# A ring of gathered rows with four hands in place of three, in a graph and attention layer

## The chip, the cores and the metric

The kernel runs on one core of a Trainium2 chip. The metric is the device time of one execution in microseconds (us). The kernel before has a median of 1078.74 us over three runs.

## The reference

The layer takes 3125 nodes with 256 features and 53,125 weighted edges, and it adds three things to `x`:

```
xn = layernorm(x)
x  = x + segment_sum(w * xn[dst], src) @ W.T + b    # edges: a gather, a sum by node, a product
       + mix(xn)                                    # linear attention over all nodes, norm, MLP, norm
x  = x + ffn(layernorm(x))                          # the two best of eight experts, then a norm
```

The attention needs a sum over all nodes (keys by values) before any node can be finished, so it has two passes over the nodes.

## The kernel before

**Tiles.** The nodes are 25 tiles of 128 rows. `x` stays in SBUF as `X`. The work has four stages. First the normalised rows times `W.T` are written to DRAM as `xg_dram`, while TensorE, VectorE, ScalarE and GpSimd sort the edges by target tile. The sort leaves a table of 444 columns (`COLS`). A column is a chunk: up to 128 edges whose targets lie in one tile. `SIX` holds the row of `xg_dram` for each edge, `SLO` the target's place in its tile and `SW` the weight. The first pass over the nodes (loop A, 13 steps of a pair of tiles, the last of one tile) and the second (loop B, the same) follow, and last comes the expert stage.

**The chunks ride along.** The 444 chunks are worked off beside loops A and B, with 18 chunks to a step (a round), which is three hands of six (`HAND`, `HANDS`, `RC`). Four engines take part:

- GpSimd issues one indirect DMA for each chunk (`gather`, line 572). It fills slot `c mod 18` of `RING`, 128 rows of 256 floats. Before it overwrites the first slot of a pair it waits for the pair of chunks that lay there 18 chunks earlier (`chunk_mm`, line 578). It does nothing else in loops A and B.
- VectorE makes a selection matrix `SEL` for each chunk (`select`), two hands ahead.
- TensorE multiplies `SEL` by the ring's slot (`hand`, line 1511, the product at line 1523). Two chunks share a PSUM bank, and the pairs alternate between banks 6 and 7. A hand waits until its six gathers have landed (`gathered[h]`) and until its `SEL` is there. A pair waits until VectorE has added the last pair but one to `X` (`x_added`).
- VectorE adds each product to its tile of `X` (`add`, line 1057), in the order of the chunks.

**Order of work.** Each engine has a fixed program order, and the hands stand between the parts of the loops. In loop B TensorE's step is: hand 0, the second projection of the step before (`b_project`), two pairs of hand 1, the attention of the next step (`b_attend`), the last pair of hand 1, a transpose, hand 2, and the hidden layer (`b_hidden`, line 1607). So whatever delays one of these delays all that stands behind it on TensorE, and ScalarE and VectorE wait for their inputs from it.

**Queues.** The gathers are issued by GpSimd on a queue of their own. SyncE loads the experts' first weights, one expert after each full round of chunks (`sp.wait_ge(chunk_mm[0], (e + 1) * (RC // 2))`, line 473).

Of the kernel before, what the change touches and what calls it, by code (L numbers as in the profile page):

```python
# [5 lines left out]
def gps_layer_program(nc, x, row, col, weight, gnn_wT, gnn_b, qkv_wT, ln1_g, ln1_b, mix_w1T, mix_b1,  # L6
# [12 lines left out]
    P = 128  # L19
    N, C = out.shape  # L20
# [21 lines left out]
    assert CQ <= P and CH <= P // 2 and QS4 * TILES <= 512 and 2 * SETS * TILES + TILES <= 512 and NG // 2 * TILES <= 512  # L42
    HAND = 6
    HANDS = 3
    RC = HANDS * HAND
    ROUNDS = 2 * PAIRS
    COLS = -(-(EK + TILES - 1) // HAND) * HAND
    TAIL = COLS // HAND - ROUNDS * HANDS
    assert TAIL == 2 and COLS <= 512
# [9 lines left out]
    with ctx:  # L59
        def sb(name, shape, dt=f32):  # L60
            return scope.enter_context(nc.sbuf_tensor(name, shape, dt))

        def sem(name):
            return ctx.enter_context(nc.semaphore(name))
# [51 lines left out]

        BID = sb("BID", [1, ROUNDS + 1, -(-RC // 4) * 4], i32)
        VX = sb("VX", [P, 2, CC, VE])
# [61 lines left out]
        scope.close()  # L180
        scope = until_ffn
        QT = sb("QT", [P, CC, TILES * P])
        RING = sb("RING", [P, RC, C])
        SEL = sb("SEL", [P, 2, HAND, P])


# [56 lines left out]
        bank = [ctx.enter_context(nc.psum_tensor(f"bank{n}", [P, 512], f32)) for n in range(8)]  # L243
# [50 lines left out]
        table_done = sem("table_done")  # L294
        slots_ready = sem("slots_ready")
        x_biased = sem("x_biased")
        gathered = [sem(f"gathered{h}") for h in range(HANDS)]
        sel_ready = sem("sel_ready")
        chunk_mm = [sem(f"chunk_mm{s}") for s in range(2)]
        x_added = sem("x_added")  # L300
# [137 lines left out]
        def _(sp):  # L438
# [33 lines left out]
            for e in range(NE):  # L472
                sp.wait_ge(chunk_mm[0], (e + 1) * (RC // 2))
                sp.dma_start(FW1A[:, e, :, :], exp_w1[e, :, :].rearrange("(c p) f -> p c f", p=P)).then_inc(up_in, 16)
# [21 lines left out]
        def _(pool):  # L496
# [74 lines left out]

            def gather(c):

                r, at = divmod(c, RC)
                k = at % HAND
                if r and k % 2 == 0:
                    pair = (c - RC) // 2
                    pool.wait_ge(chunk_mm[pair % 2], pair // 2 + 1)
                pool.indirect_dma_start(RING[:, at, :], None, xg_dram,  # L579
                                        bass.IndirectOffsetOnAxis(ap=SIX[:, c:c + 1], axis=0)  # L580
                                        ).then_inc(gathered[at // HAND], 16)
# [4 lines left out]
            for c in range(COLS):  # L586
                gather(c)
# [249 lines left out]
        def _(dve):  # L837
# [119 lines left out]
            def column_buckets():  # L957
                dve.wait_ge(bid_sum, 1)
                whole = ROUNDS * RC
                chain.link(V.tensor_scalar(BID[0:1, 0:ROUNDS, 0:RC], bank[6][0:1, 0:whole].rearrange("p (r c) -> p r c", c=RC),  # L960
# [98 lines left out]
            def hand(base, r, h, ks=range(HAND)):  # L1059

                t = r * HANDS + h
                for k in ks:
# [310 lines left out]
        def _(pe):  # L1373
            T = nc.tensor
# [11 lines left out]
            for b in range(TILES):  # L1386
                pe.wait_ge(oh_made, b + 1)
                for s in range(QS4):
                    ins = T.matmul(bank[6][0:CQ, s * TILES + b:s * TILES + b + 1], OH[:, b, s * CQ:(s + 1) * CQ], onesb[:, 0:1],
                                   start=True, stop=True)  # L1390
# [30 lines left out]
            for s in range(QS4 - 1):  # L1421
                lo, n = 2 * (s + 1), SETS - 2 * (s + 1)
                sets = CNT[0:CQ, s:s + 1, :].to_broadcast([CQ, n, TILES])
                for kind in range(2):
                    at = (kind * SETS + lo) * TILES
# [85 lines left out]
            def hand(r, h, js=range(HAND // 2)):  # L1511

                t = r * HANDS + h
                for j in js:
                    pair = t * (HAND // 2) + j
                    if j == 0:
                        pe.wait_ge(sel_ready, t + 1)
                        pe.wait_ge(gathered[h], r * (16 * HAND) + 16 * HAND)
                    if pair >= 2:
                        pe.wait_ge(x_added, 2 * (pair - 1))  # L1520
                    for u in range(2):
                        k = 2 * j + u
                        ins = T.matmul(bank[6 + pair % 2][:, u * C:(u + 1) * C], SEL[:, t % 2, k, :], RING[:, h * HAND + k, :],  # L1523
                                       start=True, stop=True)
                    ins.then_inc(chunk_mm[pair % 2], 1)

# [37 lines left out]
            for i in range(PAIRS):  # L1564
                a_transpose(i, (0, 1))
                hand(i, 0)
                a_project(i, (0, 1))
                hand(i, 1)
                hand(i, 2)
                a_outer(i, (0, 1))  # L1570
# [111 lines left out]
            for c in range(CC):  # L1682
                ins = T.matmul(bank[5][:, 2 * NE + c:2 * NE + c + 1], MEANR[0:1, c * P:(c + 1) * P], ones[0:1, 0:1], start=True, stop=True)
            ins.then_inc(mean_turned, 1)
            pe.wait_ge(mean_col, 1)
            for c in range(CC):
                ins = T.matmul(bank[5][0:1, 0:NE], MEAN[:, c:c + 1], RW[:, c, :], start=(c == 0), stop=(c == CC - 1))
# [104 lines left out]
```

## Time and profile before

| | us |
|---|---|
| runs of the kernel before | 1075.21, 1078.74, 4162.33 |
| median | 1078.74 |
| the profiled execution's own time | 1080.07 |
| its span, first to last instruction | 1078.2 |
| gathers, first to last issue | 211.7 to 871.6 |
| GpSimd busy, of the span | 571.1 (53%) |
| TensorE busy, of the span | 814.6 (76%) |
| VectorE busy, of the span | 674.9 (63%) |
| granted TensorE clock, mean | 0.882 |

Times of rows are counted from the start of the span. A row of the timeline gives start, length, engine and line, what is written and read, and in brackets how long the engine had been idle and what ended that. "remote" there means that the profile saw a semaphore's wait end and found no instruction that ended at that moment; on one core no other core can be meant. The ends of TensorE's matmuls are modelled in this profile, and their starts are recorded. PE is TensorE, PEld its weight loads, DVE is VectorE, ACT is ScalarE and POOL is GpSimd. One product of a chunk is two MATMUL records.

### The profile page before, as it was taken

The page shows a single profiled execution, that of the slowest core. Times are in us where ns is not written, and L with a number is a line of the kernel's source. Part 1 is how long each engine was busy: PE and PEld are TensorE (multiplying, and loading weights), DVE is VectorE, ACT ScalarE, POOL GpSimd, SP SyncE. Part 2 cuts the span into 40 slices and gives each one's busy share as a digit, 9 for nine tenths or more (in the row PEclk, how much of TensorE's full clock was granted, in tenths as well). Part 3 has the DMA queues.
Part 4 walks back from the last instruction along what each step waited for, and adds up shares of the span by engine and source line. Part 5 has one row for each costly group of instructions (what it writes and reads, how often), then busy time and mean ns, then how long its engine had stood idle before and what let it go on. Part 6 is the DMA issues. An engine that isn't in the chain of part 4 may idle for free.

```text
span 1078.2 us, 14388 instructions
## 1 busy us (share of the span) xinstructions
PE 814.6 (76%) x4349; PEld 648.0 (60%) x4349; DVE 674.9 (63%) x1932; ACT 375.3 (35%) x909; POOL 571.1 (53%) x624
## 2 busy tenths in 40 slices
PE   5887999845776686667666667666676778999997
PEld 4666899633554454445445555555555563899997
DVE  8888888514444454445445666666666677976685
ACT  1548999310211221111112222222222234756552
POOL 3824444276666666666665666666666620243342
PEclk9988999967979878887878888888888899999999
DMA  8110000032324332333332333333233440100000
GB/s 234 60 64 1 1 0 0 10 103 87 107 83 117 88 110 86 109 91 112 91 105 74 109 92 108 88 88 87 84 88 88 81 42 1 51 25 26 20 26 28
DMA packets 39177, 77.29 MB, mean 72 GB/s; under 512 B 9875, under 2 KB 22600, under 8 KB 39112
## 3 DMA queue, kind: packets, MB, share of 16 engines
q0 software_dynamic: 21312, 58.22, 19.8%
q1 hardware_dynamic: 17800, 18.29, 5.4%
q8 instruction: 30, 0.49, 0.2%
q14 instruction: 35, 0.29, 0.1%
HBM read 70.00 MB, written 6.48 MB: 71 GB/s over the span
## 4 chain that ended last, share of the span: by engine, by line
PE 44%; DVE 19%; another core or an unknown queue 19%; issue 11%; ACT 3%; DVEq 1%; POOL 1%; DMA 1%; SPq 0%; POOLq 0%; ACTq 0%
PE bank L1696 12%; PE bank L1486 9%; PE bank L1523 9%; DVE X L1057 8%; PE bank L1545 2%; PE bank L1618 2%; DVE SEL L1045 2%; PE bank L1404 1%; DVE ST L862 1%; PE bank L1377 1%; PE bank L1492 1%; PE bank L1493 1%; PE bank L1665 1%; PE bank L1621 1%
## 5 line engine op out<-in xcount | busy, mean ns | idle before, releaser
L579 POOL DMA_INDIRECT RING<-xg_rows,SIX x444 | 429.2, 967 | 246.5 <-issue 119.3
L1523 PE MATMUL bank<-RING,SEL 128*128 128x256 f32 x888 | 270.8, 447 | 191.9 <-DVE X L1057 153.6
L1057 DVE TENSOR_TENSOR X<-bank,X 128x256 f32 x444 | 187.2, 422 | 303.1 <-remote 205.7
L1523 PEld LDWEIGHTS bank<-RING,SEL 128*128 128x128 f32 x888 | 183.6, 220 | 257.7 <-DVE X L1057 187.3
L1045 DVE TENSOR_SCALAR SEL<-iota,SLO,SW 128x128 f32<-128x128 f32 x444 | 151.4, 343 | 0.0
L1486 PEld LDWEIGHTS bank<-OI,AS 128*128 128x128 f32 x832 | 97.4, 196 | 14.6 <-DVE AS L1014 9.5
L1486 PE MATMUL bank<-OI,AS 128*128 128x128 f32 x832 | 97.6, 279 | 8.8 <-DVE AS L1014 8.8
L566 POOL TENSOR_TENSOR AS<-LH,EPC 128x832 f32<-128x832 f32 x32 | 50.0, 1582 | 72.3 <-DVE LH L1006 72.3
L704 ACT ACTIVATE NK<-bank 128x256 f32<-128x256 f32 x25 | 9.7, 387 | 158.4 <-remote 127.8
L663 ACT ACTIVATE LD<-iota,LANE 128x128 f32<-128x128 f32 x208 | 62.5, 387 | 4.4 <-DVE LANE L994 4.0
L827 ACT ACTIVATE HF<-bank,FB 128x256 f32<-128x256 f32 (+1 forms) x104 | 49.5, 476 | 39.4 <-PE bank L1696 35.6
L1696 PE MATMUL bank<-QH,W1L 128*128 128x256 f32 (+1 forms) x208 | 59.5, 286 | 1.7 <-DVE W1L L1280 1.7
L597 POOL TENSOR_TENSOR RS<-VE,mhalf 128x1 f32<-128x1 f32 x25 | 15.5, 618 | 82.4 <-DVE VE L1330 82.4
L1696 PE MATMUL bank<-QH,W1H 128*128 128x256 f32 (+1 forms) x208 | 58.6, 282 | 0.0
L1696 PE MATMUL bank<-QL,W1H 128*128 128x256 f32 (+1 forms) x208 | 58.6, 282 | 0.0
L1696 PE MATMUL bank<-W2H,HFL 128*128 128x256 f32 x200 | 56.7, 283 | 0.0
L1696 PE MATMUL bank<-W2L,HFH 128*128 128x256 f32 x200 | 56.4, 282 | 0.0
L1696 PE MATMUL bank<-W2H,HFH 128*128 128x256 f32 x200 | 56.3, 282 | 0.0
L1545 PE MATMUL bank<-QKVW,XT 128*128 128x512 f32 x100 | 54.8, 698 | 0.0
L592 POOL TENSOR_TENSOR XN<-XN,B2C 128x256 f32<-128x256 f32 x25 | 20.0, 801 | 63.1 <-DVE B2C L1311 63.1
L1318 DVE TENSOR_TENSOR HFL<-HF,HFH 128x256 fp32r<-128x256 f32 (+1 forms) x104 | 47.6, 506 | 4.8 <-ACT HFH L827 4.2
L697 ACT COPY XT<-bank 128x512 f32<-128x512 f32 (+1 forms) x13 | 7.4, 569 | 121.7 <-remote 87.1
(273 smaller groups left out, 1491.0 us busy)
## 6 DMA issues: line engine op xcount, KB each, us to landing
RING<-xg_rows,SIX POOLq DMA_INDIRECT x444
FW1A<-in_exp_w SPq DMA_DIRECT2D x8, 512.0 KB
xg_rows<-XGS SPq DMA_DIRECT2D x12, 256.0 KB, 2.1
out<-YO SPq DMA_DIRECT2D x24, 128.0 KB, 1.7
X<-in_x SPq DMA_DIRECT2D x1, 1664.0 KB, 12.7
X<-in_x SPq DMA_DIRECT2D x1, 1536.0 KB, 8.3
FW<-in_exp_w SPq DMA_DIRECT2D x2, 512.0 KB, 4.5
QKVW<-in_qkv_wT SPq DMA_DIRECT2D x1, 768.0 KB
```

What stands on the lines that cost most here:

```text
L566: pool.tensor_tensor(AS[:, s, :, LC:2 * LC], LH[:, s, :, :], per_chunk(EPC, i, s, LC), ALU.mult).then_inc(ap_ready, 1)
L579: pool.indirect_dma_start(RING[:, at, :], None, xg_dram, bass.IndirectOffsetOnAxis(ap=SIX[:, c:c + 1], axis=0)).then_inc(gathered[at // HA ...
L663: ins = act.activation(LD[:, k, :], iota[:, :], ACT.Abs, scale=-1.0, bias=LANE[:, bass.ds((4 * i + s) * GC + k, 1)])
L827: ins = act.activation(into, bank[s][:, 0:width], ACT.Gelu, bias=FB1[:, n // FJ, n % FJ:n % FJ + 1])
L1045: ins = V.tensor_scalar(SEL[:, t % 2, k, :], iota[:, :], SLO[:, at], SW[:, at], ALU.is_equal, ALU.mult)
L1057: V.tensor_tensor(xt, bank[6 + pair % 2][:, half * C:(half + 1) * C], xt, ALU.add).then_inc(x_added, 1)
L1318: V.tensor_tensor(HFL[par][:, n, 0:width], HF[:, s, 0:width], HFH[par][:, n, 0:width].bitcast(f32), ALU.subtract).then_inc(hl_ready, 1)
L1486: ins = T.matmul(bank[s][:, 0:P], AS[:, s, k, :], OI[:, s, k, :], start=(k == 0), stop=(k == GC - 1))
L1523: ins = T.matmul(bank[6 + pair % 2][:, u * C:(u + 1) * C], SEL[:, t % 2, k, :], RING[:, h * HAND + k, :], start=True, stop=True)
L1545: ins = T.matmul(bank[2 + s][:, :], XT[:, c, s, :], QKVW[:, c, C:3 * C], start=(c == 0), stop=(c == CC - 1))
L1618: T.matmul(bank[3 + s][:, 0:C], HS[:, h, s, :], W2[:, h, :], start=(h == 0), stop=False)
L1696: ins = T.matmul(into, left, right, start=(m == 0), stop=(m == len(terms) - 1))
```

## The change

The ring gets a fourth hand: `RING` has 24 slots (24 KB in each partition) in place of 18. The hands of a round stay three, so hand `t` now lies in part `t mod 4` of the ring, and `gathered` becomes four semaphores. The gather of chunk `c` waits for the pair that held its slots 24 chunks earlier. SyncE's waits, `SEL`, the PSUM banks, the pairs and the order of work on every engine stay as they are.

```
     HAND = 6
     HANDS = 3
+    HELD = 4
     RC = HANDS * HAND
...
-        RING = sb("RING", [P, RC, C])
+        RING = sb("RING", [P, HELD * HAND, C])
...
-        gathered = [sem(f"gathered{h}") for h in range(HANDS)]
+        gathered = [sem(f"gathered{h}") for h in range(HELD)]
...
             def gather(c):
-                r, at = divmod(c, RC)
-                k = at % HAND
-                if r and k % 2 == 0:
-                    pair = (c - RC) // 2
+                lap, at = divmod(c, HELD * HAND)
+                if lap and at % 2 == 0:
+                    pair = (c - HELD * HAND) // 2
                     pool.wait_ge(chunk_mm[pair % 2], pair // 2 + 1)
                 pool.indirect_dma_start(RING[:, at, :], None, xg_dram,
...
             def hand(r, h, js=range(HAND // 2)):
                 t = r * HANDS + h
+                lap, held = divmod(t, HELD)
                 for j in js:
                     pair = t * (HAND // 2) + j
                     if j == 0:
                         pe.wait_ge(sel_ready, t + 1)
-                        pe.wait_ge(gathered[h], r * (16 * HAND) + 16 * HAND)
+                        pe.wait_ge(gathered[held], (lap + 1) * 16 * HAND)
...
-                        ins = T.matmul(bank[6 + pair % 2][:, u * C:(u + 1) * C], SEL[:, t % 2, k, :], RING[:, h * HAND + k, :],
+                        ins = T.matmul(bank[6 + pair % 2][:, u * C:(u + 1) * C], SEL[:, t % 2, k, :], RING[:, held * HAND + k, :],
                                        start=True, stop=True)
```

## Rows read from the trace of the kernel before

**Rows 1.** The page, part 1: busy us (share of the span) x instructions
```profile
PE 814.6 (76%) x4349; PEld 648.0 (60%) x4349; DVE 674.9 (63%) x1932; ACT 375.3 (35%) x909; POOL 571.1 (53%) x624
```

**Rows 2.** Waits, GpSimd's: us in total, times, longest us
```profile
POOL RING L579 <- issue: 119.3, 391, 0.5
...
POOL RING L579 <- remote: 67.5, 30, 4.1
...
POOL RING L579 <- PE bank L1523: 44.8, 22, 8.8
```

**Rows 3.** Line 579, the gathers: ns min/median/max, first and last start us
```profile
L579 POOL DMA_INDIRECT RING<-xg_rows,SIX x444: 940/946/1922, 211.7 to 871.6; - x148
```

**Rows 4.** Waits, TensorE's: the two on the ring's products
```profile
PE bank L1523 <- DVE X L1057: 153.6, 54, 13.2
...
PE bank L1523 <- DMA RING<-xg_rows,SIX: 8.5, 1, 8.5
```

**Rows 5.** Windows of line 579: stretch, its us, busy us (x gathers begun)
```profile
205.00:231.60 26.60, 15.32 (x16) 0.74 0.27 72
...
205.00:331.20 126.20, 81.28 (x83) 0.80 0.32 89
...
205.00:738.10 533.10, 344.50 (x356) 0.83 0.33 96
```

**Rows 6.** Windows of line 1523: the same stretches, PE busy (x matmuls)
```profile
205.00:231.60 26.60, 5.46 (x12) 3.96 (x13) 0.74 0.27 72
...
205.00:331.20 126.20, 45.52 (x144) 31.02 (x145) 0.80 0.32 89
...
205.00:738.10 533.10, 210.48 (x684) 143.74 (x685) 0.83 0.33 96
```

**Rows 7.** Timeline: the first product that reads the ring
```profile
221.20 5.46 PE L1523 MATMUL bank<-RING,SEL 128*128 128x256 f32 x12 [8.52 <-DMA RING<-xg_rows,SIX]
```

**Rows 8.** Timeline: the first long stall, in loop A
```profile
229.96 1.89 PE L1552 MATMUL bank<-XT,QKVW 128*128 128x256 f32 x8
...
231.68 1.89 PE L1523 MATMUL bank<-RING,SEL 128*128 128x256 f32 x8
...
236.46 0.38 ACT L704 ACTIVATE NK<-bank 128x256 f32<-128x256 f32 x1 [7.09 <-remote]
...
240.86 0.95 POOL L579 DMA_INDIRECT RING<-xg_rows,SIX  x1 [0.30 <-issue]
245.59 0.60 ACT L716 ACTIVATE NQ<-bank 128x512 f32<-128x512 f32 x1 [6.29 <-remote]
...
245.89 0.94 POOL L579 DMA_INDIRECT RING<-xg_rows,SIX  x1 [4.08 <-remote]
```

**Rows 9.** Timeline: one round of loop B
```profile
719.05 0.94 POOL L579 DMA_INDIRECT RING<-xg_rows,SIX  x1 [2.61 <-remote]
...
728.88 0.94 POOL L579 DMA_INDIRECT RING<-xg_rows,SIX  x1 [2.43 <-PE bank L1523]
...
735.45 1.13 PE L1523 MATMUL bank<-RING,SEL 128*128 128x256 f32 x4 [0.34 <-issue]
...
741.08 0.42 DVE L1057 TENSOR_TENSOR X<-bank,X 128x256 f32 x1 [3.71 <-remote]
...
742.61 0.94 POOL L579 DMA_INDIRECT RING<-xg_rows,SIX  x1 [0.30 <-issue]
...
746.01 0.84 ACT L752 ACTIVATE HS<-bank,B1C 128x256 f32<-128x256 f32 x2 [10.26 <-remote]
...
746.30 0.94 POOL L579 DMA_INDIRECT RING<-xg_rows,SIX  x1 [2.75 <-remote]
```

**Rows 10.** Windows, loop B: us, PE, PEld, DVE, ACT, POOL busy (x), clock, DMA
```profile
592.00:872.00 280.00, 193.43 (x788) 148.32 (x786) 179.17 (x652) 63.34 (x106) 178.10 (x187) 0.85 0.35 91
```

**Rows 11.** Timeline: the last gather, and the last two adds
```profile
871.61 0.94 POOL L579 DMA_INDIRECT RING<-xg_rows,SIX  x1 [0.30 <-issue]
...
889.33 0.98 DVE L1057 TENSOR_TENSOR X<-bank,X 128x256 f32 x2 [0.20 <-DVE X L1057]
```

More of the change, by code:

```diff
@@ L44, in gps_layer_program @@
     HANDS = 3
+    HELD = 4
     RC = HANDS * HAND
@@ L182, in gps_layer_program @@
         QT = sb("QT", [P, CC, TILES * P])
-        RING = sb("RING", [P, RC, C])
+        RING = sb("RING", [P, HELD * HAND, C])
         SEL = sb("SEL", [P, 2, HAND, P])
@@ L296, in gps_layer_program @@
         x_biased = sem("x_biased")
-        gathered = [sem(f"gathered{h}") for h in range(HANDS)]
+        gathered = [sem(f"gathered{h}") for h in range(HELD)]
         sel_ready = sem("sel_ready")
@@ L572, in gather @@
             def gather(c):
[L574 to L577, printed above, removed]
+                lap, at = divmod(c, HELD * HAND)
+                if lap and at % 2 == 0:
+                    pair = (c - HELD * HAND) // 2
                     pool.wait_ge(chunk_mm[pair % 2], pair // 2 + 1)
@@ L1513, in hand @@
                 t = r * HANDS + h
+                lap, held = divmod(t, HELD)
                 for j in js:
@@ L1517, in hand @@
                         pe.wait_ge(sel_ready, t + 1)
-                        pe.wait_ge(gathered[h], r * (16 * HAND) + 16 * HAND)
+                        pe.wait_ge(gathered[held], (lap + 1) * 16 * HAND)
                     if pair >= 2:
@@ L1522, in hand @@
                         k = 2 * j + u
-                        ins = T.matmul(bank[6 + pair % 2][:, u * C:(u + 1) * C], SEL[:, t % 2, k, :], RING[:, h * HAND + k, :],
+                        ins = T.matmul(bank[6 + pair % 2][:, u * C:(u + 1) * C], SEL[:, t % 2, k, :], RING[:, held * HAND + k, :],
                                        start=True, stop=True)
```

## The prediction, made blind

> **What bounds the kernel now.** I read the busy times first. No engine is full over the span: TensorE 76%, VectorE 63%, GpSimd 53% [rows 1]. The change touches only the 660 us in which gathers are issued [rows 3], so that stretch has to be read alone. In loop B's part of it TensorE is busy 193.4 us of 280, VectorE 179.2 and GpSimd 178.1 [rows 10]. Nobody is full there either, so waits set the pace and the question is who waits for whom.
>
> GpSimd's waits come next. Its gathers take 0.946 us each [rows 3] and follow each other after 0.30 us, 119.3 us in 391 gaps [rows 2]. That is 1.25 us a gather and 444 x 1.25 = 555 us for all. The other 67.5 + 44.8 = 112.3 us are waits before a gather [rows 2], and the only wait in the gathers' code is the one for a free pair of slots. So GpSimd runs into a full ring 52 times. This is the wait that the change moves.
>
> Then I read what the ring's reader waits for. TensorE has waited for a gather once, 8.5 us, at the very first hand [rows 4]. Its other wait on these products is for VectorE's adds, 153.6 us in 54 times [rows 4]. The reader is late and the ring is full.
>
> How full can be counted. At 231.6 us 16 gathers had begun and TensorE had begun 12 matmuls, which is 6 chunks; 16 - 6 = 10 chunks lay in the ring or were on their way [rows 5, 6]. At 331.2 us it was 83 - 72 = 11, and at 738.1 us 356 - 342 = 14 [rows 5, 6]. These are moments at which a new hand begins, when the need is greatest. The need is six chunks that have landed. The sixth gather began near 211.7 + 5 x 1.25, some 218 us, and the first product started at 221.20 [rows 3, 7], so landing costs about 3 us, or some 2.3 gathers. A hand can start at a level of 8 to 9. After the first hand the level was 10, 11 and 14 at these three points. The ring of 18 already has more than its reader asks for.
>
> Last, why the reader is late. There are long stalls that the profile calls "remote". The query product of loop A was begun at 229.96 and its records last 1.89 us, yet ScalarE, which waits for it, starts at 245.59; GpSimd gets its slots at 245.89 [rows 8]. In loop B a pair's product begins at 735.45 and VectorE adds it at 741.08; the hidden layer behind it reaches ScalarE at 746.01, after 10.26 us of idle time, and GpSimd again resumes 0.29 us later [rows 9]. So TensorE's news arrives late, by up to 14 us, and everything behind it waits. These stalls are on the path and the empty slots are not. The Trainium skill ("Perfetto Trace Analysis", section "Tensor Engine Instruction (MATMUL, LD_WEIGHTS)") says that the end shown for a matmul is an estimate from its size and that the semaphore is raised only when PSUM has acknowledged the data. The rows agree so far as the consumers start long after the estimated ends; what holds the news back they do not say.
>
> **The change, part by part.** The waits for a slot fall from (444 - 18) / 2 = 213 to (444 - 24) / 2 = 210. A wait that is satisfied shows no cost, the gathers after one follow at the same 0.30 us, so this is 0. The fourth semaphore and the other index are fixed in the code and add no instruction: 0. The gathers' number, size and queue are the same, and DMA is busy 0.35 of the stretch [rows 10]: 0. The adds, products and selections keep their order: 0. SyncE's loads wait for the same counts of pairs, so they start at the same point of the work.
>
> The gathers move ahead by six chunks, 6 x 1.25 = 7.5 us, from the 25th on. Until then nothing differs. In steady state the ring is filled, GpSimd stops, and it is restarted by a pair's completion. With 24 slots the same completion frees the slots of a gather six places further on. Every level is then six higher and each distance to full is as before. In loop B GpSimd resumes at 719.05 after 2.61 us, at 728.88 after 2.43 and at 746.30 after 2.75 [rows 9]. From 719.05 to 746.30 is one round of 18 gathers with two stops, 27.25 us, where 18 x 1.25 = 22.5 would do. I expect the same stops at the same places. The reader's chain sets the 27.25, and it does not get shorter when the writer is further ahead.
>
> Two places are not steady. **At the start**: GpSimd issued its 24th gather at 240.86, stopped at 241.81 and was released at 245.89 [rows 8]. The new ring lets it go on for 7.5 us, to about 249.3. If the stall ends by itself, this costs nothing. But ScalarE, VectorE and GpSimd all got their news 2.5 to 4.1 us after GpSimd had fallen silent, here and in the stalls of loop B (742.61 + 0.94 = 743.55, released at 746.01) [rows 8, 9]. If the news comes only when the gathers pause, this stall lasts 7.5 us longer. ScalarE did get one piece at 236.46 with GpSimd running [rows 8]. So the bounds are 0 and +7.5 us, one release speaks for each, and I take the middle, +3.8. **At the end**: the last gather would be issued 7.5 us earlier than 871.6 measured by TensorE's work, and the last 18.7 us of products and adds [rows 11] become some 26. They take what the reader takes. The last 7.5 us of gathers may have delayed it by something between 0 and 2.4 us (one short stop [rows 9]); I take 0. A ring-full pause of GpSimd itself costs nothing where its reader is late: its cover is the level of 10 or more.
>
> The sum is 1080.07 + 3.8 = 1083.9 us for the profiled execution. That execution lies 1.3 us above the median of 1078.74, so the forecast for the median is 1082.5, say 1082 us.
>
> **The rivals.** A measurement of this kernel tells about 2%, 21.6 us, from no change.
>
> *Faster: the ring's depth is what is missing.* For it speaks that GpSimd stands 112.3 us at a full ring [rows 2] and that TensorE seems able to do a round in less than 22.5 us: 27.25 less the 10.26 us idle time before ScalarE's hidden layer [rows 9] is 17. If the stalls were rare and a deeper ring bridged them, GpSimd's 555 us would be the bound and the time 1080 - 112 = 968 us. Against it: to bridge a reader's stall helps the writer only, and the reader has the ring's content before it, after, and during the stall. It decides only where the level would otherwise fall under 8. The Trainium skill ("Perfetto Trace Analysis", section "Optimization Strategy") has a rule for this side: the same gap coming back on the engine that should be saturated can mean that there are too few buffers. By that rule the 52 stops would be paid back, and the time would be this rival's; the wait of 8.5 us, once, on TensorE is what the trace holds against it. Chance 12%. In between, a part of loop A's uneven rounds could fall better by luck.
>
> *Slower: every long stall lasts until the larger ring is full.* GpSimd was released by "remote" 30 times [rows 2]. If the stalls end only when the gathers pause, and if each now begins with more free slots than before, each grows by up to 7.5 us. Three of them cross the line of 21.6 us; ten rounds of loop B alone would cost 75 us and give 1155. For it speak the 2.5 to 4.1 us between GpSimd's last issue and the release. Against it: a stall in loop B begins at a level of 14, four gathers from full (356 gathers had begun at 738.1, and the fourth after them is the one at 742.61) [rows 5, 9], because the stop before 728.88 had filled the ring shortly before. With 24 slots that stop fills it too, and the stall again begins four gathers from full. The point that decides is whether the stop in the middle of the round remains. Chance 10%.
>
> *The change doesn't do what it says*, the gathers keep waiting at the old distance: then 1080 and no difference. The index and the wait both use 24, so I give it no chance of its own; it would land in the forecast's band.
>
> **How the numbers follow.** The forecast, no change beyond 2% (1057 to 1100 us), has 78%, faster 12%, slower 10%. The unknown costs are 0 and +7.5 at the start and 0 to -2.4 at the end, 1076 to 1086 by themselves. Loop A's stalls are irregular, with stops of 1.5 to 4.1 us, and a shift may move some of them, three or four either way, another 15 us. That makes 1061 to 1101. The range 1060 to 1103 leaves out the far cases of both rivals and takes in their near ends.
>
> **What would show it.** GpSimd's first stop should move from before the 25th gather to before the 31st. TensorE should again wait for a gather once, for 8.5 us. The level at the start of a hand should be 16 to 20 in place of 10 to 14. GpSimd's waits at a full ring should stay near 112 us less 7.5, and a round of loop B should stay 27.25 us with two stops. The first release of ScalarE's line 716 tells the two bounds apart: 245.6 or about 253. The forecast is wrong if loop B's round falls towards 22.5 us, or if the stalls in it grow by several us each.

## The result, and the profile after

The changed kernel takes **1085.59 us** (median of four runs, 1085.12 to 1087.68). The kernel before has one more run beside these, of 1069.01 us. Its median over all four is 1076.97, and without the execution that stalled at 4162 us, which the comparison leaves out, it is 1075.21. The ratio is 1.0094, with a 95% interval of 1.0060 to 1.0129. That is no change by the 2% bound, and slower by about 10 us by the interval. A second timing, told below, agrees: 1.0088 (1.0054 to 1.0122). All ratios compare executions in the faster of the two states that kernels show here; of the late reader with 24 slots, below, one execution of four (1203.03 us) is in the slow state and is left out, and it is the one that was profiled.

The profiled execution took 1085.12 us with a span of 1083.4, where before's took 1080.07 with 1078.2. Busy times from the page, to be read beside [rows 1]:

```profile
span 1083.4 us, 14388 instructions
...
PE 817.3 (75%) x4349; PEld 650.5 (60%) x4349; DVE 674.6 (62%) x1932; ACT 375.4 (35%) x909; POOL 572.5 (53%) x624
```

The work is the same on each engine, so the difference is in the waits. From the view of waits (us in total, times, longest), which answers to [rows 2, 4]:

```profile
PE bank L1524 <- DVE X L1057: 173.4, 56, 21.3
...
POOL RING L579 <- remote: 66.3, 26, 4.9
...
POOL RING L579 <- PE bank L1524: 41.1, 22, 5.6
...
PE bank L1524 <- DMA RING<-xg_rows,SIX: 8.5, 1, 8.5
```

GpSimd waits 66.3 + 41.1 = 107.4 us at a full ring in 48 stops, against 112.3 in 52. TensorE waits for a gather once, for the same 8.5 us. But its longest wait for an add has grown from 13.2 to 21.3 us, and the total by 19.8.

The levels, from the windows of line 579 (stretch, its us, busy us, x gathers begun), as in [rows 5]:

```profile
205.00:340.00 135.00, 88.13 (x91) 0.77 0.33 92
205.00:742.00 537.00, 350.42 (x361) 0.83 0.33 96
```

and of the products of line 1524, as in [rows 6]:

```profile
205.00:340.00 135.00, 46.15 (x144) 32.20 (x144) 0.77 0.33 92
205.00:742.00 537.00, 211.85 (x684) 145.05 (x684) 0.83 0.33 96
```

At the same counts of products as before, 72 and 342 chunks, the ring now holds 91 - 72 = 19 and 361 - 342 = 19 chunks. Before it held 11 and 14. (The windows close 0.5 and 0.7 us before the hand starts; at its start the second level is 20.) Counted at the start of each hand of a settled round of loop B, the levels go from 18, 16 and 14 to 24, 22 and 20. The lowest level after the first hand, as long as gathers are still to come, was 10 and is 10, both times at the second hand. The ring is fuller, and nobody needed it.

A round of loop B, from the timeline (start, us, engine, line, idle time before), to be laid beside [rows 9]:

```profile
723.53 0.95 POOL L579 DMA_INDIRECT RING<-xg_rows,SIX  x1 [2.51 <-remote]
...
733.42 0.94 POOL L579 DMA_INDIRECT RING<-xg_rows,SIX  x1 [2.50 <-PE bank L1524]
...
747.18 0.94 POOL L579 DMA_INDIRECT RING<-xg_rows,SIX  x1 [0.30 <-issue]
...
750.40 0.84 ACT L752 ACTIVATE HS<-bank,B1C 128x256 f32<-128x256 f32 x2 [10.11 <-remote]
750.70 0.94 POOL L579 DMA_INDIRECT RING<-xg_rows,SIX  x1 [2.57 <-remote]
```

From 723.53 to 750.70 is 27.17 us with two stops, where before it was 27.25 with two stops. ScalarE's stall is 10.11 us for 10.26. GpSimd's last issue ends at 748.12, and the hidden layer starts 2.3 us later.

The first stall of loop A, from the timeline, against [rows 8]. First a line of before that [rows 8] does not show, the first add of the second hand:

```profile
245.75 0.42 DVE L1057 TENSOR_TENSOR X<-bank,X 128x256 f32 x1 [17.65 <-remote]
```

and then the changed kernel:

```profile
229.15 1.89 PE L1524 MATMUL bank<-RING,SEL 128*128 128x256 f32 x8
...
232.21 0.38 ACT L704 ACTIVATE NK<-bank 128x256 f32<-128x256 f32 x1 [5.38 <-remote]
...
245.55 0.94 POOL L579 DMA_INDIRECT RING<-xg_rows,SIX  x1 [0.30 <-issue]
249.70 0.60 ACT L716 ACTIVATE NQ<-bank 128x512 f32<-128x512 f32 x1 [14.63 <-remote]
...
251.24 0.42 DVE L1057 TENSOR_TENSOR X<-bank,X 128x256 f32 x1 [25.98 <-remote]
251.37 0.95 POOL L579 DMA_INDIRECT RING<-xg_rows,SIX  x1 [4.88 <-remote]
```

This is where the time went. The products of the second hand start at 229.15 and their first add at 251.24, which is 22.1 us. Before, the same two points lie at 231.68 and 245.75, 14.1 us apart. GpSimd issues until 246.49, six chunks further than before, and the news of TensorE's products reaches ScalarE, VectorE and GpSimd 3.2 to 4.9 us after that.

In the rest of the stage the differences nearly cancel. I read each round as the time from its first add to the next round's first add. Round 0 goes from 38.9 to 47.9 us (+9.0). Rounds 1 to 11 go from 285.3 to 281.6 (-3.7), round 12 changes by -0.6, rounds 13 to 23 by +1.9, and the last adds by +1.1. From the first product on the ring (221.20, now 218.35) to the last pair of adds (889.33, now 894.15) the stage is 7.7 us longer. The part ahead of it was 2.85 us shorter in this execution, so the span grew by only 5.2. Single rounds of loop A differ by up to 8.8 us either way, so the -3.7 is scatter: the second profile of the changed kernel, told below, has +9.2 in round 0, +0.7 in rounds 1 to 11, +0.5 in round 12, +2.0 in rounds 13 to 23 and +1.1 at the end.

### The profile page after: what moved, and what is told of

It reads as the page before. It is cut to its first block, busy times and chain, and to the rows that moved or that the text cites. A ratio compares the mean times of both kernels' runs of the same rounds, so it can differ in the third digit from the quotient of the medians.

```text
span 1083.4 us, 14388 instructions
## 1 busy us (share of the span) xinstructions
PE 817.3 (75%) x4349; PEld 650.5 (60%) x4349; DVE 674.6 (62%) x1932; ACT 375.4 (35%) x909; POOL 572.5 (53%) x624
## 4 chain that ended last, share of the span: by engine, by line
PE 40%; another core or an unknown queue 20%; DVE 19%; issue 13%; ACT 4%; DVEq 1%; POOL 1%; DMA 1%; SPq 0%; POOLq 0%; ACTq 0%
PE bank L1697 12%; PE bank L1486 9%; DVE X L1057 9%; PE bank L1524 8%; DVE SEL L1045 2%; PE bank L1377 1%; DVE ST L862 1%; PE bank L1404 1%; PE bank L1492 1%; PE bank L1493 1%; PE bank L1546 1%; PE bank L1619 1%; PE bank L1666 1%; PE bank L1622 1%
## 5 line engine op out<-in xcount | busy, mean ns | idle before, releaser
L592 POOL TENSOR_TENSOR XN<-XN,B2C 128x256 f32<-128x256 f32 x25 | 20.1, 802 | 73.2 <-DVE B2C L1311 73.2
L827 ACT ACTIVATE HFH<-bank,FB 128x256 fp32r<-128x256 f32 (+1 forms) x104 | 49.8, 479 | 0.0
```

The costliest lines, as they stand in the source:

```text
L592: pool.tensor_tensor(XN[:, tile(t)], XN[:, tile(t)], B2C[:, :], ALU.add).then_inc(res_ready, 1)
L827: ins = act.activation(into, bank[s][:, 0:width], ACT.Gelu, bias=FB1[:, n // FJ, n % FJ:n % FJ + 1])
```

## The experiments

The theory after the result (**A**): while GpSimd issues gathers back to back, the news that TensorE has finished is held back. It comes through when GpSimd stops, and what stops it is the full ring. So the one stall that begins with the ring far from full lasts as long as it takes to fill the ring, and a deeper ring makes it longer. The rivals: **B**, the new layout or the fourth semaphore costs the time; **C**, the DMA traffic of the gathers delays the news; **D**, TensorE is itself late and "remote" is only how the profile names it. "News" is here the completion of a product as the engines that wait for it see it.

**Distance alone.** The layout of the change stays, but the gathers wait at 18 chunks as before:

```diff
-                if lap and at % 2 == 0:
-                    pair = (c - HELD * HAND) // 2
+                if c >= RC and at % 2 == 0:
+                    pair = (c - RC) // 2
```

> The changed kernel with its ring of 24 slots and its four semaphores, but each gather waits for the pair 18 chunks earlier, as before the change. Theory A (TensorE's completions reach nobody while GpSimd issues gathers back to back, and come through some 2.5 us after it stops): only the distance counts, so GpSimd stops before the 25th gather, the first long stall from the product of pair 3 to its add is again 14 us and not 22, and the time is that of the kernel before, 1077 us, ratio 1.00. Rival B (the stalls are TensorE's own and the 8 us come from where the tensors lie in SBUF or from the fourth semaphore): the time stays at 1085 us, ratio 1.009, and the first stall at 22 us.

Measured: 978.44 us (975.01 to 981.85), ratio 1.0012 (0.9992 to 1.0032) to the kernel before, which took **978.59 us** on this chip in 29 runs (974.42 to 981.79). A hundred us were gone without an edit. The view of waits shows what is different on this chip:

```profile
DVE X L1057 <- PE bank L1524: 202.3, 100, 8.5
POOL RING L579 <- issue: 131.1, 430, 0.3
...
PE bank L1524 <- DMA RING<-xg_rows,SIX: 37.9, 12, 8.4
```

The gathers run through at their own pace: 430 gaps of 0.30 us, and no stop at a full ring is among the waits. None of the adds waits for "remote". GpSimd's issuing is the bound here, 444 x 1.25 = 555 us, and TensorE now waits for gathers 12 times. The ring never fills, so none of the four kernels that were timed on this chip could show what a deeper ring costs.

**Distance 14**, `c >= 14` and `(c - 14) // 2` in the same place, same chip:

> The changed kernel, but each gather waits for the pair 14 chunks earlier. Theory A: GpSimd stops four gathers (5 us) sooner than before the change, so the first stall is 14 - 5 = 9 us and the time some 1072 us, ratio 0.995, unless the level at the start of a hand (10 to 14 before, now 6 to 10, where 8 to 9 are needed) makes TensorE wait for gathers; then waits on the ring's DMA appear and the time goes up, to about 1090. Rival B: the first stall keeps its 14 or 22 us, and the time is 1077 to 1085 us or, with starvation, more.

Measured: 979.95 us, ratio 1.0018 (0.9998 to 1.0038). With the writer as the bound a distance of 14 chunks is enough. It says nothing on A, and this distance was not run on a chip that has the stalls.

**An earlier first stop.** The kernel before, in which the 19th and the next gathers wait for pair 4:

```diff
-                    pair = (c - RC) // 2
+                    pair = max((c - RC) // 2, 4)
```

> The kernel before, with 18 slots, but the gathers 18, 20, 22 and 24 all wait for pair 4, so that GpSimd falls silent after its 18th gather, at about 233 us, where it went on to the 24th. Theory A: TensorE's news comes some 2.5 us after that, the first stall ends at about 236 in place of 245.6, and the time falls by up to 9 us to 1068 to 1072, ratio 0.992 to 0.996. Rival B: the release stays at about 245.6, the gathers start again later than they did (245.6 with 18 issued in place of 24), and the time is 1077 us or more, ratio 1.00 or above.

Measured: 977.07 us, ratio 0.9994 (0.9973 to 1.0015). There is no stall on this chip, so there is nothing to shorten.

**The copies on SyncE.** The changed kernel with the same ring, waits and bytes, but plain DMAs from SyncE's queue. They read the 128 rows of one tile and leave the indices out, so this kernel does not compute the layer. GpSimd issues nothing in the stage, and the experts' weights are issued from the same place in SyncE's program as the copies. The main part of the edit:

```diff
-                pool.indirect_dma_start(RING[:, at, :], None, xg_dram,
-                                        bass.IndirectOffsetOnAxis(ap=SIX[:, c:c + 1], axis=0)
-                                        ).then_inc(gathered[at // HAND], 16)
+                sp.dma_start(RING[:, at, :], xg_dram[bass.ds((c % TILES) * P, P), :]).then_inc(gathered[at // HAND], 16)
```

> The gathers leave GpSimd. SyncE issues a plain DMA of the same size in their place (128 rows of 1 KB, rows of a fixed tile: the indices are left out, so this part of the work is not computed), with the ring of 24 slots and the same waits; the experts' weights are issued in the same queue at about the same points. If it is GpSimd's issuing that holds TensorE's news (theory A in its narrow form): no stall is left, a round of loop B falls from 27.25 to under 20 us, and the time falls by 150 us or more, to below 930 us. If it is the DMA traffic into SBUF that holds it: the stalls stay with traffic of the same kind, and the time stays over 1000 us. Rival B (TensorE's own stalls): the reader's chain is unchanged, 27.25 us a round, 1077 to 1086 us.

Measured: 884.19 us, ratio 0.9058 (0.9025 to 0.9091). Without the writer's bound the reader needs 94 us less even on the chip that has no stalls.

The measurements from here on, where nothing else is said, are on a second chip, on which the kernel before takes 1078.62 us, as in the first measurement.

**The change again.**

> The changed kernel as it is, timed again. In the last runs the kernel before took 978.6 us and its family showed no stall: GpSimd never stopped at a full ring and TensorE waited 12 times for gathers. Theory A (the 8 us come from a stall that lasts until GpSimd stops): where TensorE's news isn't held there is nothing to lengthen, and where GpSimd never meets a full ring the distance of its waits means nothing, so the ratio to before is 1.000 (within 0.3%) if the kernel before takes 979 us, and again 1.007 to 1.010 if it takes 1077. Rival B (the place of the tensors in SBUF or the fourth semaphore): +8 us in both, ratio 1.008.

Measured: 1088.52 us, ratio 1.0088 (1.0054 to 1.0122). From its timeline:

```profile
245.72 0.95 POOL L579 DMA_INDIRECT RING<-xg_rows,SIX  x1 [0.30 <-issue]
...
251.45 0.42 DVE L1057 TENSOR_TENSOR X<-bank,X 128x256 f32 x1 [26.29 <-remote]
251.59 0.95 POOL L579 DMA_INDIRECT RING<-xg_rows,SIX  x1 [4.91 <-remote]
```

The second hand's products start at 228.76 in it, and their first add 22.7 us later. The longer stall is no accident of one execution.

**The earlier first stop again**, the same kernel as above:

> The kernel before with GpSimd stopped after its 18th gather until pair 4 is done, once more. If the kernel before takes 1077 us here: theory A says the first stall ends at about 236 us in place of 245.6 and the ratio is 0.992 to 0.996; rival B says 1.00 or above. If it takes 979 us: no stall, ratio 1.00 for both.

Measured: 1074.82 us, ratio 0.9989 (0.9952 to 1.0026), no difference, where A had been taken to mean 0.992 to 0.996. But the stall did what A says. Timeline:

```profile
226.09 1.89 PE L1523 MATMUL bank<-RING,SEL 128*128 128x256 f32 x8
...
228.11 0.94 POOL L579 DMA_INDIRECT RING<-xg_rows,SIX  x1 [0.30 <-issue]
230.52 0.39 ACT L704 ACTIVATE NK<-bank 128x256 f32<-128x256 f32 x1 [6.75 <-remote]
...
232.14 0.42 DVE L1057 TENSOR_TENSOR X<-bank,X 128x256 f32 x1 [9.65 <-remote]
232.34 0.95 POOL L579 DMA_INDIRECT RING<-xg_rows,SIX  x1 [3.28 <-remote]
```

GpSimd falls silent at 229.05, and the add comes 3.1 us later. The stall is 6.0 us in place of 14.1, and round 0 is 29.0 us for 38.9. The next round then takes 32.3 us for 20.1, for in it the ring fills from 8 chunks to 18, and GpSimd runs without a stop for that long. The gain was given back at once. So the cost is not that of one stop. It is that of filling the ring: the gathers that are issued ahead of the reader are issued while the reader's news is held. It is paid once, sooner or later, and six chunks more are 6 x 1.25 = 7.5 us more. That it is paid once is argued from this one round, among rounds of loop A that scatter by as much.

**The distance again**, the same kernel as in the first experiment, on a third chip (the kernel before: 1076.26 us):

> The changed kernel with its ring of 24 slots, but each gather waits for the pair 18 chunks earlier, once more. Theory A, where the kernel before takes 1077 to 1079 us: the first long stall is again 14 us and not 22, and the ratio is 1.000 and not 1.009. Rival B (the tensors' places, the fourth semaphore): ratio 1.009, as for the changed kernel. Where it takes 979 us, 1.00 for both.

Measured: 1073.55 us, ratio 0.9974 (0.9945 to 1.0003). Timeline:

```profile
225.85 1.89 PE L1524 MATMUL bank<-RING,SEL 128*128 128x256 f32 x8
...
235.41 0.94 POOL L579 DMA_INDIRECT RING<-xg_rows,SIX  x1 [0.30 <-issue]
...
240.20 0.42 DVE L1057 TENSOR_TENSOR X<-bank,X 128x256 f32 x1 [17.95 <-remote]
240.34 0.94 POOL L579 DMA_INDIRECT RING<-xg_rows,SIX  x1 [3.99 <-remote]
```

With all of the new layout and the old distance the stall is 14.4 us again and the loss is gone. B is out. The distance makes the difference. (The full distance was not timed on this third chip. Where it was, in two timings, it cost 0.9%.)

**The copies on SyncE again**, on the second chip:

> SyncE's plain DMAs in place of GpSimd's gathers once more (indices left out, so this part is not computed). On the chip where the kernel before took 979 us this ran in 884 us. Theory A, narrow form (GpSimd's issuing holds TensorE's news): no stall, so 884 us also where the kernel before takes 1077, a ratio of 0.82. If the traffic into SBUF holds it, whoever issues: stalls in every round, over 1000 us, ratio 0.93 or more. Rival B (TensorE's own stalls): about 1077 us, ratio near 1.0.

Measured: 884.62 us, where before takes 1079.32, ratio **0.8203** (0.8171 to 0.8235). It is the same 884 as on the fast chip. Its longest waits at the ring (SPq is SyncE's own queue, which stands at a full ring):

```profile
SPq L482 <- PE bank L1521: 247.5, 143, 7.2
...
DVE X L1054 <- PE bank L1521: 103.5, 57, 6.3
...
PE bank L1521 <- DVE X L1054: 58.6, 74, 3.1
...
PE bank L1521 <- DMA RING<-xg_rows: 4.6, 1, 4.6
```

And the stage in one window (us, busy PE, PEld, DVE, ACT, POOL with counts, granted clock, DMA share, GB/s):

```profile
215.00:690.00 475.00, 394.93 (x1716) 292.79 (x1715) 358.28 (x1229) 133.10 (x265) 0.00 (x0) 0.98 0.43 129
```

against the same of the kernel before:

```profile
215.00:872.00 657.00, 442.67 (x1668) 322.11 (x1668) 349.88 (x1188) 127.42 (x256) 425.97 (x442) 0.83 0.34 95
```

Nearly the same bytes (61 and 62 MB) move at 129 GB/s for 95, and the DMA engines are busier, 0.43 for 0.34. Yet no wait of any engine is put down to "remote", and the longest wait of a product for an add is 3.1 us for 13.2. More traffic and no held news: C is out as far as the amount of traffic goes. What TensorE, VectorE and ScalarE do is unchanged, so D is out too, in the sense that TensorE is not late by itself. What is left is the gathers as GpSimd issues them. The run changes several things of them at once and does not part them: the issuing engine, the kind of DMA (indirect and, by the page, `software_dynamic` before; direct and `hardware_dynamic` here), the rows read, and the rhythm, for SyncE stops at a full ring 143 times. TensorE's clock goes with it: it is granted 0.98 of full speed in this stretch in place of 0.83, where it had stood still for about 10 us in each round. For the same 4349 matmuls of the whole kernel TensorE is busy 754.4 us by the page, where it was 814.6 [rows 1]. That is at most 60 of the 195 us, and waits are the rest. Seen another way, 94 of the 195 us are gained also on the chip where nothing is held, by lifting the writer's 555 us bound. That leaves about 100 us for the held news, an estimate, as it sets two chips side by side.

**A late reader, with 18 and with 24 slots.** In loop A before the query product and in loop B before the hidden layer, 14 more matmuls into a bank that nobody reads, in the kernel before and in the changed one:

```diff
+                for _ in range(14):
+                    T.matmul(bank[5][:, 0:COLS], zeros[:, :], iota_c[:, :], start=True, stop=True)
```

> The kernel before with a reader that is late on purpose: 14 matmuls on zeros (128x444, 0.74 us each at the full clock, some 10 us) ahead of the query product in each step of loop A and ahead of the hidden layer in each step of loop B. 26 steps x 10.3 us on top of the 884 us that the reader took with SyncE's copies make some 1150 us. Theory A: GpSimd now meets a full ring in every round, levels near 18. Rival C (a deeper ring is worth something to a late reader) and theory A differ in the next run.

> The changed kernel, with the same 14 matmuls in each step. Theory A: with the reader late and its ring full, every level is six higher, the stops are the same, and the time is that of the late reader with 18 slots within 0.3%, where news isn't held, and at most 8 us more where it is. Rival C: the six more slots save GpSimd's stops at a full ring, and the time falls by up to their sum, several per cent.

Measured: 1182.09 us, ratio 1.0964 (1.0929 to 1.0998) with 18 slots, and 1182.33 us, the median of the three executions that count, 1.0968 (1.0911 to 1.1025) with 24. GpSimd's longest kind of stop, with 18 slots:

```profile
POOL RING L579 <- PE bank L1523: 185.9, 39, 15.2
```

and with 24 (the profile of the execution that was left out):

```profile
POOL RING L579 <- PE bank L1524: 191.3, 38, 14.1
```

The extra products keep TensorE busy for 221 us more (1036.0 for 814.6 with 18 slots), and the time grows by about 103. The later reader finds the same ring full, 12 chunks or more at the start of every hand but the first and the last, and gets nothing from a deeper one. GpSimd merely stands longer at either distance.

**An uneven distance**, on the same chip. If the loop B stall were tied to one place in the round, stops placed ahead of it would let the news through. The changed kernel, with a distance of 14 at chosen pairs of each round and 24 at the others:

```diff
-                if lap and at % 2 == 0:
-                    pair = (c - HELD * HAND) // 2
+                near = (c - 14) // 2
+                held_at = (0, 1, 8) if near >= 9 * PAIRS else (0, 1, 3, 4)
+                pair = near if near % 9 in held_at else (c - HELD * HAND) // 2
+                if pair >= 0 and at % 2 == 0:
```

> The changed kernel with uneven distances: a gather waits for the pair 14 chunks earlier where that pair is one at which the long stalls begin (in loop B the pairs 9r+8, 9r and 9r+1, in loop A 9r, 9r+1, 9r+3 and 9r+4), and 24 chunks earlier elsewhere. Theory A: GpSimd falls silent when a stall begins and not four gathers (5 us) later, and the stop in the middle of the round (2.4 us) goes, since the ring isn't full then. A round of loop B falls from 27.25 to about 25 us (18 x 1.25 for the gathers and one stop of 2.5), loop A gains about as much, and the time falls by 20 to 50 us, to 1030 to 1060, where the kernel before takes 1077. Rival: each stall saved is given back in the next one until the ring is full, as after the early first stop, and the time stays within 1077 to 1086. Where the kernel before takes 979 us, the ratio is 1.00 for both.

Measured: 1172.37 us (1165.24 to 1177.14), ratio 1.0847 (1.0800 to 1.0893), a plain miss of both expectations. The timeline of a round of loop B shows why:

```profile
833.60 1.99 PE L1526 MATMUL bank<-RING,SEL 128*128 128x256 f32 x8
...
844.83 0.94 POOL L581 DMA_INDIRECT RING<-xg_rows,SIX  x1 [0.30 <-issue]
849.07 0.42 DVE L1059 TENSOR_TENSOR X<-bank,X 128x256 f32 x1 [14.72 <-remote]
...
859.28 0.95 POOL L581 DMA_INDIRECT RING<-xg_rows,SIX  x1 [13.50 <-PE bank L1526]
```

The stall isn't at the hidden layer any more but at the products of the round's second hand. It lasts until GpSimd stops at 845.77, and the news is there 3.3 us later. Then GpSimd waits 13.5 us for a near pair, because it had run so far ahead. A round takes 35.5 us in place of 27.2. The stall has no place of its own. It begins with something that TensorE finishes while GpSimd is running, and here it ends with GpSimd's next stop. Counted from the trace, GpSimd issues 18 gathers without a stop in each settled round of loop B here, where the kernel before and the changed one issue 12 and 6. So long runs without a stop are the dear ones.

**A pause after each hand.** If stops are what lets news through, short ones that need no full ring should pay. The kernel before, with two fills of an unused tile after every sixth gather:

```diff
                 gather(c)
+                if c % HAND == HAND - 1 and c < COLS - 2 * HAND:
+                    for _ in range(2):
+                        chain.link(pool.memset(apart[:, :], 0.0))
```

> The kernel before, and after each six gathers (but the last two hands) GpSimd does two memsets of 128x400, each waited for, some 1.0 to 1.3 us in all. Theory A and the rows of loop B, where six gathers followed by a stop of 2.6 us pass without a stall and a stall begins within some 7 us after the next restart: if 1 us without a gather is enough to let TensorE's news through, no long stall is left, GpSimd sets the pace with 74 x (7.5 + 1.2) = 644 us less what it no longer stops for, and the time falls by 15 to 45 us, to 1035 to 1062. If it isn't enough, the stalls stay, GpSimd reaches a full ring later and each stall gets longer by the memsets in it, and the time is 1077 to 1095. Where the kernel before takes 979 us, GpSimd is the bound and the memsets cost 72 x 1.2 = 86 us less the slack of TensorE's waits: 1040 to 1065.

Measured, on the third chip: **1061.90 us** (1059.58 to 1063.54), ratio 0.9865 (0.9831 to 0.9898). It is the fastest of the kernels with gathers on the chips where before takes 1076 to 1079 us, though GpSimd is busy for 64 us more by the page (634.8 for 571.1). Its waits:

```profile
DVE X L1060 <- remote: 145.6, 54, 8.7
...
PE bank L1526 <- DVE X L1060: 93.2, 55, 6.5
...
PE bank L1526 <- DMA RING<-xg_rows,SIX: 24.1, 5, 8.3
```

The longest held add is 8.7 us, and TensorE's waits for adds are 93.2 us in place of 153.6. The first stall is gone: the second hand's products start at 226.19 and their first add at 227.36. GpSimd's full-ring waits for "remote" fall from 67.5 us in 30 times to 15.7 in 12. GpSimd is at work in these pauses, so what counts is the runs of gathers and not whether the engine is busy. ScalarE's waits for "remote" fall from 340 us to 184, about half. The time falls by 14 us only, for the pauses also slow the writer: the ring now holds 7 to 9 chunks at the start of over half of loop A's hands, and TensorE waits for gathers 24.1 us in 5 times in place of 8.5 once. The kernel was not run on the chip where before takes 979 us; there the fills would lengthen the engine that sets the pace.

**How far A reaches.** From the first gather to the first stop GpSimd issues 18 gathers with the early stop, 20 with the uneven distance, 24, 24, 30 and 30 in the other four profiles with stalls above. From the second hand's product to its first add it takes 6.0, 8.4, 14.1, 14.4, 22.1 and 22.7 us. The longer the run, the longer the stall, and each ends 3.1 to 4.8 us after the last gather of the run. But A as stated above is too strong for the whole kernel. In the trace of the kernel before, VectorE and ScalarE stand for over 4 us until a "remote" 46 times while the gathers last. 28 of these waits, 261 of 424 us, end while GpSimd stands. The other 18 end while it is issuing, as this one does, 11.4 us after GpSimd had started again at 350.97:

```profile
362.32 0.58 ACT L697 COPY XT<-bank 128x512 f32<-128x512 f32 x1 [8.80 <-remote]
362.70 0.95 POOL L579 DMA_INDIRECT RING<-xg_rows,SIX  x1 [0.30 <-issue]
```

So many stalls end with a stop of GpSimd, and some end without one. What ends those was not found.

## Why the prediction was right, and what was off

**Right: the steady state does not change.** It said that every level would be six higher, with the same stops, and a round of loop B would stay 27.25 us. Measured in loop B were 24, 22 and 20 chunks for 18, 16 and 14, two stops of 2.5 us and 27.17 us. (It named 10 to 14 before and 16 to 20 after, from three hands. Over all hands but the first two and the last three the levels were 11 to 18 and are 17 to 24.) GpSimd's full-ring waits were to be near 112 less 7.5, which is 105; they were 107.4. The wait of 8.5 us for a gather came back once.

**Right in kind, mis-sized: the stall at the start.** This is the term that moved the time. The prediction gave it 0 to +7.5 us, by whether the stall ends by itself or when the gathers pause, and took the middle, +3.8. The view that it named to decide was the first release of line 716, 245.6 or about 253 by the old start. It came at 249.70. Because this execution started the ring's stage 2.85 us earlier, that is 252.6 on before's axis, so the upper bound. From product to add it is 8.0 us more, over the whole stage 7.7. The two timings give +10.4 us and +9.9 us for the medians, with about 4 us of uncertainty, where the sum had +3.8. The forecast of 1082 was 3.6 us low, and most of that is this term. That it came so near owes something to luck: the forecast took 1078.74 as its base, and with the run that came later the base is 1075.21; and the profiled execution, 1085.12 for 1083.9, had a first part that was 2.85 us shorter. The middle of two bounds was a hedge, and the runs stand at the upper one. The right reading stood in the rows already: three consumers got their news 2.5 to 4.1 us after GpSimd fell silent [rows 8, 9], in both loops. Against it stood ScalarE's one piece at 236.46, which arrived with GpSimd running. Such pieces exist in the changed kernel too (232.21 above): some news comes through, the next is held. One that comes through is no evidence against the hold.

**The end, and a place that the sum did not have.** The end was put at 0, within 0 and -2.4 us, and shows nothing clear: the last full round and the last adds together change by about +0.5 us. But one round of loop B that the prediction counted as steady, the second after the change of loops, is 30.3 us in the changed kernel and 29.2 in its second timing. It is 26.4 in the kernel before, 26.5 with the early stop and 26.4 with the new layout at the distance of 18. GpSimd's stop there, before 626.36, lasts 5.6 us. So this round costs 2.8 to 3.8 us more with the larger distance, of which rounds 13 to 23 together keep 1.9 and 2.0. I take it for the same effect, the fuller ring after a change of the round's shape, but nothing was run on it alone.

**The faster rival** (968 us, the ring's depth is missing) is refuted by the measured time and by the levels above, and the late reader fits: its ratio to the kernel before is 1.0964 with 18 slots and 1.0968 with 24. The prediction cited a rule beside it, from the Trainium skill ("Perfetto Trace Analysis", section "Optimization Strategy"): a gap that keeps coming back on the engine that should be saturated can mean too few buffers. It does not help here, for GpSimd stood at a full ring 48 times with a third more buffers, at +0.9%. A time near 968 did occur, the 978 us of the chip without held news. There GpSimd's 555 us are the bound, as the rival had it, but no deeper ring leads there.

**The slower rival** (every stall lasts until the larger ring is full) had the right mechanism for the stalls that a stop ends. It failed on the ground given against it: in loop B the stall begins a few gathers from full with either ring, because the stop in the middle of the round remains. The uneven distance took that stop away. It shows the kind of cost that the rival meant, 1172 us where 1155 was worked out, but it is no test of that number, for it also makes GpSimd wait up to 13.5 us for the near pairs.

**What stays open.** Why the news is held is not shown, only with what it comes: gathers issued by GpSimd, back to back, on some chips and not on one. The same rows do not tell the issuing from the DMA that it starts, nor a late signal from a product that is itself finished late, as the ends of TensorE's matmuls are modelled. Plain DMAs issued by GpSimd would tell the kind of DMA from the issuing engine, and were not run. The changed kernel at its full distance was never timed on the chip where before takes 979 us; the expectation that it makes no difference there rests on the distances 14 and 18, which made none. Whether a pause of another length or at another place gives more than 1.35% wasn't tried.

## What to carry to other kernels

A ring is worth its depth only where its reader ever finds it empty: count the level at the points of need (written so far less read so far) before adding slots. Where a writer with spare time stands at a full ring, ask what its stops do for others before taking them away; here many of them were the moments at which the others' news arrived, and adding short ones paid 1.35% while a longer first run without one cost 0.9%. And a wait whose releaser had long been done is a question of its own, to be put by moving the suspected engine's work elsewhere. That experiment left the indices out, so it is a bound and no version to use, but it showed 195 us, where the best that was done on the ring showed 14.

## What the runs showed of the hardware that was not expected

- **Completions of TensorE can be held while GpSimd issues gathers back to back.** The first stall, from product to add, was 14.1, 14.4, 22.1 and 22.7 us for distances of 18, 18, 24 and 24 chunks, 6.0 us with the early stop and 1.2 us with pauses. In the rows shown the news came 2.3 to 4.9 us after GpSimd's last issue; 18 of 46 long stalls of the kernel before ended while it was issuing. With plain copies of the same size issued by SyncE no wait is put down to "remote", and no product waits longer than 3.1 us for an add. The Trainium skill ("Perfetto Trace Analysis", section "Tensor Engine Instruction (MATMUL, LD_WEIGHTS)") has the semaphore raised by PSUM's acknowledgement and names nothing of GpSimd there; by these rows the time at which a product's news is seen depends on what GpSimd does.
- **It depends on the chip.** The kernel before takes 978.59 us on one chip (29 runs, 974 to 982) and 1076 to 1079 us on others, while the variant with SyncE's copies takes 884.19 us on that fast one and 884.62 on the second. The difference goes with the held news: in the profiles taken on the fast one, of three variants of the kernel, no wait of any engine is put down to "remote". The kernel before itself was timed there and not profiled. The stalls were seen in the first measurement and on the second and the third chip.
- **The granted clock goes down with the stalls.** TensorE's granted clock over the stage is 0.83 with them and 0.98 with SyncE's copies. The late reader, which keeps the gathers on GpSimd and gives TensorE 14 matmuls more where it had stood, has 0.96 from 215 to 980 us. So a wait that is removed can be paid back a second time in the work around it.
